# Joining the two transposing transfers of an attention chunk, with rings of three slots and unrolled loops

## What is computed

```python
x = x + xattn(layernorm(x), ctx_512)     # 16 heads, keys = values = rotated context (2, 4096, 128)
x = x + mix(layernorm(x))                # products of heads inside each token, no softmax
x = x + ffn(layernorm(x))                # 512 -> 1408 -> 512, int32 weights, silu(gate) * up
```

```python
q_r = rope(q @ w_kc_q) @ W_qr;  k_r = kv_r @ W_kr
attn = softmax(q_r @ k_r.T)              # 256 rows x 4096 keys
ctx = attn @ kv_r
```

## Time and profile before

| | before |
|---|---|
| median of 3 runs | 1251.05 us (1246.34 to 1253.56) |
| profiled execution, its own time | 1246.37 us |
| its span | 1244.6 us |
| TensorE, matmuls | 1126.4 us, 91% of the span |
| VectorE | 1010.3 us, 81% |
| ScalarE | 696.3 us, 56% |
| GpSimd | 430.2 us, 35% |
| DMA queue of SP (q1) | 169.17 MB, 68.2% of 16 engines' span |
| mean granted clock of TensorE | 0.974 |

### The profile page before, as it was taken

How to read it: one execution, slowest core, us unless ns; L and a number is a source line. 1 busy time by engine, 2 the same in 40 slices (tenths; PEclk the granted TensorE clock), 3 DMA queues, 4 the chain that set the end, 5 groups by cost and what they waited for, 6 DMA issues and landing times.

```text
span 1244.6 us, 26549 instructions
## 1 busy us (share of the span) xinstructions
PE 1126.4 (91%) x9080; PEld 839.0 (67%) x9080; DVE 1010.3 (81%) x1190; ACT 696.3 (56%) x1033; POOL 430.2 (35%) x377
## 2 busy tenths in 40 slices
PE   4999998999999999999999999999998879875678
PEld 3555556788887888878777777777775634333657
DVE  3887778899999899898888888888884479996933
ACT  1222237687877777777777777777774331212412
POOL 1993451243343222221222221222221158784300
...
DMA  8443308999999999999999999999997510040000
GB/s 301 140 144 100 96 22 128 170 179 181 177 179 181 177 180 180 178 180 164 175 185 182 183 184 185 182 183 183 185 182 152 110 69 0 1 185 1 1 17 18
DMA packets 562111, 174.83 MB, mean 140 GB/s; under 512 B 543264, under 2 KB 549408, under 8 KB 561952
## 3 DMA queue, kind: packets, MB, share of 16 engines
q1 hardware_dynamic: 560464, 169.17, 68.2%
...
## 4 chain that ended last, share of the span: by engine, by line
SPq 49%; PE 26%; issue 10%; DVE 8%; POOL 4%; DMA 2%; ACT 2%; DVEq 0%; ACTq 0%; POOLq 0%
SPq L330 23%; SPq L327 23%; PE ps_o L1207 4%; PE ps_o L1103 3%; PE ps_s L1078 3%; POOL prod L492 2%; PE ps_s L1261 2%; DMA pt_hi<-p_hi 1%; POOL rstd L374 1%; PE ps_t L1065 1%; PE ps_o L1093 1%; PE ps_t L1066 1%; PE ps_t L1067 1%; DVE hT L996 1%; PE ps_s L1289 1%
## 5 line engine op out<-in xcount | busy, mean ns | idle before, releaser
L844 DVE SCALAR_TENSOR_TENSOR p_lo<-prob,p_hi 128x1024 f16<-128x1024 f32 x256 | 318.9, 1246 | 84.8 <-DMA pt_lo<-p_lo 66.6
L575 ACT ACTIVATE p_hi<-prob 128x1024 f16<-128x1024 f32 x256 | 270.7, 1057 | 149.3 <-DMA pt_hi<-p_hi 143.4
L582 ACT ACTIVATE prob<-ps_s,nmax 128x1024 f32<-128x1024 f32 x256 | 284.1, 1110 | 57.3 <-DVE nmax L851 54.7
L851 DVE TENSOR_REDUCE nmax<-ps_s 128x1 f32<-128x1024 f32 x256 | 311.2, 1216 | 1.8 <-PE ps_s L1159 1.8
L1170 PE MATMUL ps_o<-kn_hi,pt_hi 128*128 128x128 f16 x2048 | 260.1, 221 | 5.8 <-DMA pt_hi<-p_hi 5.5
L1171 PE MATMUL ps_o<-kn_lo,pt_hi 128*128 128x128 f16 x2048 | 257.6, 220 | 0.0
L1157 PE MATMUL ps_s<-kt_hi,q_hi 128*128 128x512 f32 x512 | 225.0, 439 | 25.1 <-ACT prob L582 22.5
L1170 PEld LDWEIGHTS ps_o<-kn_hi,pt_hi 128*128 128x128 f16 x2048 | 194.6, 98 | 75.5 <-issue 62.5
L440 POOL TENSOR_TENSOR osum<-oscl 128x256 f32<-128x256 f32 x64 | 47.3, 739 | 516.2 <-DVE oscl L880 516.2
L1159 PE MATMUL ps_s<-kt_hi,q_lo 128*128 128x512 f32 x512 | 202.5, 395 | 0.0
L1171 PEld LDWEIGHTS ps_o<-kn_lo,pt_hi 128*128 128x128 f16 x2048 | 201.8, 99 | 0.0
...
## 6 DMA issues: line engine op xcount, KB each, us to landing
...
pt_hi<-p_hi SPq DMA_TRANSPOSE x256, 3.3
pt_lo<-p_lo SPq DMA_TRANSPOSE x256, 3.3
...
```

What stands on the lines that cost most here:

```text
L575: nc.scalar.mul(p_hi[:, j % 2, :], prob[:, j % 2, :], PSCALE).then_inc(hi_done, 1)
L582: nc.scalar.activation(prob[:, j % 2, :], ps_s[:, 2 * (j % 2):2 * (j % 2) + 2, :].rearrange("p a c -> p (a c)"), ACT.Exp, bias=nmax[:, i, ...
L844: nc.vector.scalar_tensor_tensor(out=p_lo[:, j % 2, :], in0=prob[:, j % 2, :], scalar=PSCALE, in1=p_hi[:, j % 2, :], op0=ALU.mult, op1=ALU ...
L851: nc.vector.tensor_reduce(nmax[:, i, c:c + 1], ps_s[:, 2 * (j % 2):2 * (j % 2) + 2, :].rearrange("p a c -> p (a c)"), AX_X, ALU.max, negat ...
```

## The change

- One transfer per chunk: p_hi and p_lo are two parts of one tile p_both, pt_hi and pt_lo of pt_both, both with a ring of RING = 3 slots; SP waits for the lower half and issues one transposing transfer of 128 x 2048.
- Scores go to a ring of three PSUM slots of two banks: the four banks of ps_s and the two of ps_t. A slot is free when the exponents of the chunk three items before are taken. Between the last 4 chunks of batch 0, the keys of batch 1 pass through the same ring, 1024 columns at a time. The exponents stay in the two buffers of prob.
- Row sum, reciprocal and chunk weights go from VectorE to GpSimd, where the reciprocal is a power with exponent -1.
- The loops of the attention are written out on all five engines, and counters start at 0.
- The output product of tile 0, its copies and the first norm go from the last head to behind the last chunk.
- TensorE starts the scores when all keys of batch 0 are split (`kt_done` 8).

The diff, cut (left out: semaphores' names, starting values, constants of the same waits, `minus`, a tile of -1.0, and `pair_sum`):

```diff
 AHEAD = 4
-SPARE = 8
+RING = 3
...
-                p_hi = sb(st, "p_hi", [P, 2, CHUNK], F16)
-                p_lo = sb(st, "p_lo", [P, 2, CHUNK], F16)
-                pt_hi = sb(st, "pt_hi", [P, 4, CHUNK // P, P], F16)
-                pt_lo = sb(st, "pt_lo", [P, 4, CHUNK // P, P], F16)
+                p_both = sb(st, "p_both", [P, RING, 2, CHUNK], F16)
+                pt_both = sb(st, "pt_both", [P, RING, 2, CHUNK // P, P], F16)
...
+        def slot(k):
+            return ps_s[:, 2 * (k % RING):2 * (k % RING) + 2, :] if k % RING < 2 else ps_t[:, :, :]
+        def flat(banks):
+            return banks.rearrange("p a c -> p (a c)")
+        def p_hi(n):
+            return p_both[:, n % RING, 0, :]
+        def p_lo(n):
+            return p_both[:, n % RING, 1, :]
...
-            def turn_exponents(b, h, j):
-                n = b * H * NSTEP + h * NSTEP + j
-                sp.wait_ge(pv_done, SPARE + n - 3)
-                sp.sem_inc(turn_go, 1)
-                sp.wait_ge(hi_done, SPARE + n + 1)
-                sp.sem_inc(turn_go, 1)
-                sp.dma_start(pt_hi[:, j % 4], p_hi[:, j % 2, :], transpose=True).then_inc(hi_in[j % 2], 16)
-                sp.wait_ge(lo_done, SPARE + n + 1)
-                sp.sem_inc(turn_go, 1)
-                sp.dma_start(pt_lo[:, j % 4], p_lo[:, j % 2, :], transpose=True).then_inc(lo_in[j % 2], 16)
...
-            for b in range(B):
-                if b == B - 1:
+            def turn_exponents(n):
+                if n >= RING:
+                    sp.wait_ge(pv_done, n - RING + 1)
+                sp.wait_ge(lo_done, n + 1)
+                sp.dma_start(pt_both[:, n % RING].rearrange("p a c q -> p (a c) q"),
+                             p_both[:, n % RING].rearrange("p a c -> p (a c)"),
+                             transpose=True).then_inc(pt_in[n % RING], 16)
+            for n in range(NCHUNK):
...
-                with sp.Fori(0, H) as h:
-                    if b == B - 1:
-                        sp.dma_start(wmix[:, bass.ts(h, D)], w_mix[:, bass.ts(h, D)]).then_inc(wmix_in, 16)
-                    for j in range(NSTEP):
-                        turn_exponents(b, h, j)
...
+                if n >= NCHUNK // B and n % NSTEP == 0:
+                    h = n // NSTEP - H
+                    sp.dma_start(wmix[:, bass.ts(h, D)], w_mix[:, bass.ts(h, D)]).then_inc(wmix_in, 16)
+                turn_exponents(n)
...
+            def chunk_weights(t):
+                i = t % 2
+                pool.wait_ge(al_done, t + 1)
+                nc.gpsimd.tensor_tensor(junk[:, i, :], alpha[:, i, :], rsum[:, i, :], ALU.mult).then_inc(row_ok, 1)
+                pool.wait_ge(row_ok, 3 * t + 1)
+                nc.gpsimd.tensor_tensor(pair_sum[:, :], junk[:, i, 0:2], junk[:, i, 2:4], ALU.add).then_inc(pair_ok, 1)
+                pool.wait_ge(pair_ok, t + 1)
+                nc.gpsimd.tensor_scalar(lsum[:, i, :], pair_sum[:, 0:1], pair_sum[:, 1:2], PSCALE, ALU.add,
+                                        ALU.mult).then_inc(row_ok, 1)
+                pool.wait_ge(row_ok, 3 * t + 2)
+                nc.gpsimd.tensor_tensor(lrec[:, i, :], lsum[:, i, :], minus[:, :], ALU.pow).then_inc(row_ok, 1)
+                pool.wait_ge(row_ok, 3 * t + 3)
+                nc.gpsimd.tensor_scalar(weigh[:, i, :], alpha[:, i, :], lrec[:, i, :], kunscale,
+                                        ALU.mult, ALU.mult).then_inc(weigh_ok, 1)
...
-            with pool.Fori(0, NP) as p:
-                split_query(2 * p + 2, 0)
-                sum_chunks(2 * p, 0)
-                split_query(2 * p + 3, 1)
-                sum_chunks(2 * p + 1, 1)
-                split_keys(1, p)
...
+            for t in range(NQT):
+                if t + 2 < NQT:
+                    split_query(t + 2)
+                if t:
+                    sum_chunks(t - 1)
+                chunk_weights(t)
+                if t % 2 and t // 2 < NP:
+                    split_keys(1, t // 2)
             norm_root(("x", 0))
-            sum_chunks(NQT - 2, 0)
-            sum_chunks(NQT - 1, 1)
+            sum_chunks(NQT - 1)
...
-            def take_hi(n, half, j):
-                act.wait_ge(hi_in[j % 2], 16 * SPARE + 16 * half)
-                act.wait_ge(exp_done, SPARE + n + 1)
-                nc.scalar.mul(p_hi[:, j % 2, :], prob[:, j % 2, :], PSCALE).then_inc(hi_done, 1)
...
-            def exponents(n, j):
-                act.wait_ge(m_done, SPARE + n + 1)
-                act.wait_ge(lo_done, SPARE + n - 1)
...
+            def take_hi(n):
+                if n >= RING:
+                    act.wait_ge(pt_in[n % RING], 16 * (n // RING))
+                act.wait_ge(exp_done, n + 1)
+                nc.scalar.mul(p_hi(n), prob[:, n % 2, :], PSCALE).then_inc(hi_done, 1)
+            def exponents(n):
+                act.wait_ge(m_done, n + 1)
+                if n >= 2:
+                    act.wait_ge(lo_done, n - 1)
+                i, c = n // NCH % 2, n % NCH
+                scored = flat(slot(RING_AT["chunk", n]))
+                nc.scalar.activation(prob[:, n % 2, :], scored, ACT.Exp, bias=nmax[:, i, c:c + 1], scale=1.0,
...
+            def next_keys(c):
+                act.wait_ge(ktt_done, 8 + c + 1)
+                nc.scalar.copy(kt_hi[:, c * CHUNK:(c + 1) * CHUNK], flat(slot(RING_AT["keys", c]))).then_inc(kth_done, 1)
...
-            def head(b, h, last):
-                n0 = b * H * NSTEP + h * NSTEP
-                for j in range(NSTEP):
-                    if last and b == B - 1 and j == SIDE_STEP:
-                        ctx_columns(0)
-                    exponents(n0 + j, j)
-                    take_hi(n0 + j, (b * H + h) * (NSTEP // 2) + j // 2, j)
-                    if last and b < B - 1 and j in KEY_STEPS:
-                        key_columns(b + 1, 2 * (j - KEY_STEPS[0]))
-                        key_columns(b + 1, 2 * (j - KEY_STEPS[0]) + 1)
-                    if j % NCH == NCH - 1:
-                        weights_of_chunks(b * H * TPH + h * TPH + j // NCH, j // NCH)
-            for b in range(B):
...
+            for n in range(NCHUNK):
...
-                head(b, H - 1, True)
+                exponents(n)
+                take_hi(n)
+                if ("keys", n - NCHUNK // B + NCH) in RING_AT:
+                    next_keys(n - NCHUNK // B + NCH)
+                if n % NCH == NCH - 1:
+                    weights_of_chunks(n // NCH)
...
+            ctx_columns(0)
             normalise(("x", 0))
...
-                dve.wait_ge(lo_in[j % 2], 16 * SPARE + 16 * half)
-                dve.wait_ge(hi_done, SPARE + n + 1)
...
-            def row_sum(t, i):
-                dve.wait_ge(al_done, SPARE + t + 1)
-                nc.vector.tensor_tensor_reduce(out=junk[:, i, :], in0=alpha[:, i, :], in1=rsum[:, i, :], scale=PSCALE,
-                                               scalar=0.0, op0=ALU.mult, op1=ALU.add,
...
-            def chunk_weights(t, i):
...
+            def take_lo(n):
+                dve.wait_ge(hi_done, n + 1)
...
+            def chunk_maximum(n):
+                dve.wait_ge(s_done, n + 1)
+                i, c = n // NCH % 2, n % NCH
+                if c == 0 and n >= 2 * NCH:
+                    dve.wait_ge(weigh_ok, n // NCH - 1)
...
+            def next_keys(c):
+                dve.wait_ge(kth_done, 8 + c + 1)
+                cols = slice(c * CHUNK, (c + 1) * CHUNK)
+                nc.vector.tensor_tensor(kt_lo[:, cols], flat(slot(RING_AT["keys", c])), kt_hi[:, cols].bitcast(F32),
+                                        ALU.subtract).then_inc(kt_done, 2)
...
+                dve.wait_ge(weigh_ok, t + 1)
+                dve.wait_ge(pv_done, NCH * (t + 1))
...
+            chunk_maximum(0)
+            for n in range(NCHUNK):
+                if n % NCH == NCH - 1 and n > NCH:
+                    weigh_chunks(n // NCH - 1)
+                if n + 1 < NCHUNK:
+                    chunk_maximum(n + 1)
+                take_lo(n)
+                if n % NCH == NCH - 2:
+                    row_maximum(n // NCH)
+                if ("keys", n - NCHUNK // B + NCH) in RING_AT:
+                    next_keys(n - NCHUNK // B + NCH)
+            weigh_chunks(NQT - 1)
+            layer_norm(("x", 0))
...
-                pe.wait_ge(exp_done, SPARE + n - 1)
...
+            def free_slot(k):
+                if k >= RING:
+                    kind, n = RING_ORDER[k - RING]
+                    if kind == "chunk":
+                        pe.wait_ge(exp_done, n + 1)
+                    else:
+                        pe.wait_ge(kt_done, 8 + 2 * (n + 1))
+            def scores(n):
+                k, t, c = RING_AT["chunk", n], n // NCH, n % NCH
+                free_slot(k)
+                if c == 0:
+                    pe.wait_ge(q_ready, t + 1)
+                if t % (NQT // B) == 0:
+                    pe.wait_ge(kt_done, 8 * (t // (NQT // B)) + 2 * (c + 1))
...
+            def next_keys(c):
+                k = RING_AT["keys", c]
```

(30 more changed lines are left out.)

209 lines of the change are left out of this document (64 added, 145 removed).

## The result

The changed kernel takes 1244.19 us (median of 17 runs, 1240.12 to 1246.67), the kernel before 1248.32 on the same chips (17 runs). The ratio is 0.9967, 95% interval 0.9955 to 0.9980: 4 us won where 28 were forecast.

A forecast was written before the change was run, and what follows sets the result against it. SP's queue of transposing transfers was taken as the bound. 1246.4 - 36.4 (chunks) + 2.3 (fill) + 3 (keys) + 1.4 (drain) + 4.3 (norm) = 1221.0 us, plus half of a 4.7 us offset: 1223 us, range 1206 to 1248.

The forecast's parts named there:

- Floor, bound and packets: Attention: floor is TensorE's 2.80 us a chunk, chain moves there from SP's queue; 64 code packets of 0.5 us each.
- I take 2.82 us for the first batch and 2.87 for the second: Attention: period per chunk after the change, against 2.93 and 3.05 before; 36.4 us saved.
- Slack 1.3 us, cost none in the steady state: One chunk's way from scores to weighed keys: 9.8 us needed, 11.1 available, so the longer way costs nothing.
- The gaps: SP's queue: gap before the joined transfer shrinks to 0.12 us; SP needs 2.58 us a chunk instead of 2.85.
- Issue of the joined transfer: SP's queue: one joined issue takes 2.46 us, between bounds of 1.25 and 2.50.
- rival B: SP's queue: joined issue costs far less than two, leaving TensorE's bare floor; 1212 us, or 1208; chance 12%.
- Key columns of batch 1 through the ring: Between batches: scores wait for slots holding key pieces; +3 us, bounds 0 and +6.
- First fill: Start of attention: first weighed keys start at 201.3 instead of 198.96; +2.3 us.
- Norm laid bare: After attention: tile 0's first norm, formerly covered by chunks, is now bare; +4.3 us.
- Row sums on GpSimd: Attention: moving row sums from VectorE costs GpSimd 3 to 6 us per 11.2 us tile; no effect on time.
- C: Attention: SP remains the bound, each code packet costing 0.85 us; 1250 us, no change; chance 16%.
- D: Attention: joined transfer lands 6.6 us after issue, so the three-slot ring gives period 3.10; 1288 us, slower; chance 10%.

The follow-up runs named there:

- e9: Changed kernel with TensorE's chunks in hardware loops, scores five chunks ahead, mix-weight loads at the end, four extra matmuls before the first norm: ratio 0.9745 to before.
- e3: Kernel before with only TensorE's loop over heads written out: ratio 1.0271 to the kernel before.
- e11: Changed kernel with each chunk's joined transfer split into two again: ratio 1.0062 to the kernel before.
- e16: Kernel before with SP's loop over heads written out and its three marking semaphore increments removed: ratio 0.9697 to the kernel before.
- e8: Changed kernel with TensorE's chunks in hardware loops and the mix layer's weight loads behind the last transposition: ratio 0.9787 to the kernel before.
- e1: Changed kernel without the loads of the mix layer's weights and the wait for them: ratio 0.985 to the kernel before.
- e7: Changed kernel with four extra, unread TensorE matmuls ahead of the first norm's transposes: ratio 0.9957 to the kernel before.
- e4: Changed kernel with two slots of p_both in place of three: 1423.17 us in one run.

## Why the prediction was wrong

The time lies in the range, but the size was missed: 36 us of saving in the chunks came out as 20 (128 and 124 chunks at 0.08 us each).

- **Floor, bound and packets** were right: TensorE's 2.80 us, reached in batch 1 of e9; the move of the chain to TensorE; 69 packets on q8, at 0.69 us each in e3 where 0.5 was taken; a landing of 4.6 (4.5 forecast); a gap of 3.83 us ahead of the first norm's transposes.
- **The step that failed: "I take 2.82 us for the first batch and 2.87 for the second", with "Slack 1.3 us, cost none in the steady state".** I had charged code packets and loads to SP's mean (2.71 and 2.83) and set that beside TensorE's 2.80, as if they used up SP's free time only. They lengthen single landings, up to 6.6 us where 4.5 + 1.3 = 5.8 was allowed, and what TensorE, now the bound, stands idle is not made up: 29.9 us ahead of the products in the whole run. The runs: 2.86 and 2.97; 2.82 or less in both batches once any two of packets, loads and short lead are mended. That is 15 of the 19 us missing (4.5 and 10.8 in the table).
- **The gaps.** I took SP from 2.87 us to 2.58 a chunk and gave the 0.29 to the joining and its shorter gap. With two transfers SP's list, written out, already takes 2.77 (e11, e16). The joining is then worth 0.07 of the period and 12 us (e11), and SP's own instructions alone 38 us in the kernel before (e16). I had named them ("four waits and signals with register sums") and the loop turn, without asking what they were worth alone.
- **Issue of the joined transfer:** 2.46 was taken; the median is 2.2 to 2.3, and it ranges from 1.3 to 3.9. Where a transfer stretches the landing does: with 3.2 us for 256 KB and 4.6 for 512, a landing is about 1.8 us fixed and 1.4 per 256 KB. This line through two points is an estimate. The Trainium skill's fixed cost of some 2 us ("DMA: Bandwidth & Descriptors", where the time of a DMA goes) is for transfers issued by GpSimd; the 1.8 here is of the same size. It lies in the landing, not in SP's time, so rival B did not follow from it.
- **Key columns of batch 1 through the ring:** +3 (0 to +6) was forecast. Chunks 120 to 136 took 52.05 us before and 56.02 after, though a chunk had become shorter. The versions with nearly one period tell more: the starts of products 120 and 136 in e16 (keys through banks of their own), then in e9 (through the ring):

```profile
542.71 0.61 PE L1171 MATMUL ps_o<-kn_hi,pt_lo 128*128 128x128 f16 x8
...
591.28 0.61 PE L1171 MATMUL ps_o<-kn_hi,pt_lo 128*128 128x128 f16 x8
```

```profile
547.99 0.61 PE L1185 MATMUL ps_o<-kn_hi,pt_both 128*128 128x128 f16 x8
...
603.29 0.61 PE L1185 MATMUL ps_o<-kn_hi,pt_both 128*128 128x128 f16 x8
```

  48.6 against 55.3 us, 6.7 for the ring and what stands with it. e9 starts its scores a chunk earlier, so the keys hold up a product ahead of this stretch as well. With four ahead, from product 112 (ahead of the keys) to 128, e8 takes 54.6 us and e16 48.2: 6.4 for the keys in the ring, above the upper bound of 6. It was not tried alone.
- **A load that the prediction didn't see.** ScalarE's queue loads the 1 MB of x for the residual once, in the last head before and after chunk 131 now. A transposition beside it is stretched in either place. The issue of the load and of the stretched transposition behind it, before and after, with the landings from 578 to 588 us in the changed kernel:

```profile
935.76 0.39 ACTq L625 DMA_DIRECT2D xres<-x_dram  x1
938.20 3.97 SPq L327 DMA_TRANSPOSE pt_hi<-p_hi  x1
```

```profile
578.08 0.40 ACTq L636 DMA_DIRECT2D xres<-x_dram  x1
581.07 6.12 SPq L340 DMA_TRANSPOSE pt_both<-p_both  x1
...
DMA to landing us min/median/max: 4.4/7.5/8.8
```

  The prediction counted eight stretches over 0.5 us and put them down to code; this ninth, the longest, it left out. In the changed kernel the product of chunk 130 starts 5.95 us after that of 129, so TensorE loses 3.2 us there. The stall has moved from the last head into the row of chunks 120 to 136, which is part of why that row is worse than forecast and the row from 240 on better. In e3 and e16 the load is issued at 969.9 and 900.2 us, and issues of 3.79 and 4.13 us stand right behind it there. What it costs the whole time was not tried.
- **First fill.** The first chunk starts 4.0 us later, 2.3 were forecast. From the end of the key split to the first product with the lower half it is 10.0 us before and 14.4 after, but 12.7 in e1 and e9, whose fill is the same as the changed kernel's or begins with one chunk more: 2.7 to 4.4 us, in single executions. **Norm laid bare** was 3.8 for 4.3, but the prediction had nothing for the clock behind it: 3 us, shown by e7. Another 2.3 us went in the last 47 us of the run, where the granted clock is 0.95 instead of 1.00; why is open. Row sums on GpSimd, three PSUM slots and the late load of w_dn hold up TensorE nowhere that the traces show; VectorE's lower half takes 1275 ns in the mean now, 1246 before.
- **Rivals.** C's price per packet was close, but SP is not the bound. D's landing of 6.6 us occurs as the worst case of the steady stretches, not as the median, and its ring arithmetic was borne out by e4.
